# Cross-attention and FFN kernel: K and Q transformed from sums and differences of rows t and t+64, the mixing matrix filled by DMAs

## The chip, the cores and the metric

The kernel runs on one core of one Trainium2 chip. The metric is the device time of one execution in microseconds. The kernel before takes 1065.87 us (median of 3 runs, 1065.73 to 1066.18).

## The reference

x is (128, 128, 256) and the context is (128, 128, 256), both float32; 16 heads of 16 columns, `Lv` = 128.

```python
Q, K, V = (queries @ wq), (keys @ wk), (values @ wv)     # each as (B, head, Dh, L)
corr = irfft(rfft(Q) * conj(rfft(K)), n=Lv)              # along L
top_vals, top_idx = top_k(corr, 4)
w = softmax(top_vals)
out = sum_i w[i] * V rolled by top_idx[i] along Dh (mod 16)
x = x + out @ wo                  # queries = layernorm(x), keys = values = context
x = x + ffn(layernorm(x))         # 256 -> 1024 -> 256, gelu; weights rounded to 8 bits, activations to 16
```

## The kernel before

The program is written engine by engine (one block each for SyncE, TensorE, ScalarE, GpSimd, VectorE), with semaphores between them. Every engine executes its own instructions in the written order, so that order is the schedule.

The work has three stages. Stage 1 is the attention: a loop over 64 pairs of batch elements (`PAIRS`), unrolled, software-pipelined by hand: in step t each engine calls its parts for pairs t, t-1, ... t-7 (`step(t)` on each engine), and the last pairs have an order of their own, written out after the loop. Stage 2 computes the hidden layer for 32 quads, stage 3 the output layer.

In one step of stage 1 TensorE executes, for pair n: `project_k` (L455) and `project_v` (L505), `project_out` of pair n-4 (L530), `project_q` (L468), `attend` of pair n-3 (L519), `dft_k` and `dft_q` (L481, L493), `inverse` of pair n-1 (L545). Projections are exact to more than 16 bits: both operands are split into a float16 high part and a float16 rest, and three of the four products are summed (`PARTS`). ScalarE makes the high parts, GpSimd the rests (`low_ct` for the context, `low_xt` for x, `low_cs` for the spectrum, `low_ot` for the attention's output). The two transforms are float32 matmuls with a 128 x 64 part of the table, one half of the output partitions for each batch element. The product of the spectra is formed by VectorE (`products`) and GpSimd (`add_terms`), split (`high_cs`, `low_cs`) and transformed back by 24 float16 matmuls (`inverse`).

VectorE then takes the eight largest of each row and their places (`top_values`, `top_places`), makes the mixing weights (`one_hot` to `spread_weights`) and transposes them in blocks of 32 (`turn_weights`, into `blocks`). ScalarE copies the four blocks on the diagonal into the 128 x 128 matrices of `mt` (`spread_blocks`, L749), whose other blocks stay zero, and `attend` multiplies V with them. `residual` adds x; `statistics2`, `moments2` (VectorE), `scale_both` (GpSimd) and `normalize2` (ScalarE) make the second layer norm. `scale_both` makes in one go the scale of that norm for pair t-6 and the scale of the first norm for pair t-1, which `take_q_scaled` (ScalarE) applies to Q. SyncE's queue issues the loads and stores, also in order: `store_x1`, `load_x`, `load_turned`, `load_x_turned`.

Bank 1 of PSUM holds K's projection and then Q's; bank 7 holds V's projection and then the output of `attend`.

## Time and profile before

| | |
|---|---|
| median of the runs | 1065.87 us |
| span of the profiled execution (first to last instruction) | 1064.2 us |
| stage 1, loop in steady state | one step of 8.88 us for each pair |
| stage 1, order written out for the last pairs | from 554 us to 595 us |
| stage 2, stage 3 | 595 to 821 us, 821 to 1064 us |
| busy over the span: TensorE, VectorE, ScalarE, GpSimd | 1047.4, 965.1, 939.9, 505.0 us |
| granted TensorE clock | full speed throughout |

The profiled execution's own time lies within 2 us of its span; the median of the runs is 1.7 us above the span. Busy times of matmuls are those of pipelined instructions: starts of consecutive groups say more than their durations. The chain of work that ended last is 94% TensorE.

### The profile page before, as it was taken

How to read it: one execution, taken by the hardware profiler on the slowest of the kernel's cores; microseconds unless marked ns; L12 is line 12 of the kernel's file. 1: busy time of each engine (PE TensorE's matmuls, PEld its weight loads, DVE VectorE, ACT ScalarE, POOL GpSimd, SP SyncE). 2: the span in 40 equal slices, each digit the busy share in tenths (PEclk: the TensorE clock that was granted, in tenths of full speed). 3: DMA queues.
4: the chain of work that ended last, by engine and by line, in shares of the span. 5: the costliest groups of instructions: out<-in, count | busy, mean ns of one | idle time of the engine just before them, and what ended most of it. 6: DMA issues, size and time to landing. Idle time of an engine off the chain costs nothing.

```text
span 1064.2 us, 28999 instructions
## 1 busy us (share of the span) xinstructions
PE 1047.4 (98%) x9358; PEld 778.0 (73%) x9358; DVE 965.1 (91%) x2768; ACT 939.9 (88%) x1697; POOL 505.0 (47%) x674
## 2 busy tenths in 40 slices
PE   8999999999999999999998899999999999999998
PEld 6788888888888888888887444444444888888887
DVE  4789999999988888888889999999997999999998
ACT  5888888899999998888888688888888999999996
POOL 5788888888888888888887400000001000000000
PEclk9999999999999999999999999999999999999999
DMA  5454444334445443444431498999999999999995
GB/s 178 130 150 145 121 121 120 121 120 120 121 120 140 121 120 120 121 120 120 120 111 41 132 325 301 300 305 316 309 300 342 356 347 363 355 354 355 346 364 195
DMA packets 141665, 222.59 MB, mean 209 GB/s; under 512 B 72432, under 2 KB 92272, under 8 KB 137456
## 3 DMA queue, kind: packets, MB, share of 16 engines
q1 hardware_dynamic: 140464, 220.12, 62.8%
q8 instruction: 61, 1.00, 0.4%
q10 hardware_dynamic: 1088, 1.05, 0.3%
q14 instruction: 52, 0.43, 0.1%
HBM read 121.00 MB, written 83.89 MB: 193 GB/s over the span
## 4 chain that ended last, share of the span: by engine, by line
PE 94%; ACT 2%; DVE 2%; issue 1%; DMA 1%; POOL 0%; ACTq 0%; DVEq 0%; POOLq 0%
PE sums L666 21%; PE bank L635 10%; PE sums L635 10%; PE sums L464 8%; PE sums L477 8%; PE bank L515 8%; PE sums L539 7%; PE sums L489 6%; PE bank L527 5%; PE bank L501 5%; PE bank L556 5%; PE sums L672 1%; DMA store_x<-in_L_xattn_wv 1%; ACT arena L756 0%; ACT arena L686 0%
## 5 line engine op out<-in xcount | busy, mean ns | idle before, releaser
L666 PE MATMUL sums<-wout,arena 128*128 128x256 f16 x2048 | 229.8, 273 | 1.2 <-DVE arena L1521 1.2
L666 PEld LDWEIGHTS sums<-wout,arena 128*128 128x128 f16 x2048 | 196.9, 98 | 32.5 <-DVE arena L1514 7.3
L1521 DVE SCALAR_TENSOR_TENSOR arena<-arena,wout_rel 128x512 f16<-128x512 int16 x256 | 180.3, 746 | 2.0 <-ACT arena L935 0.9
L756 ACT ACTIVATE arena<-arena 32x128 f32<-32x128 f32 x256 | 78.6, 307 | 47.8 <-DVE arena L1222 45.5
L635 PE MATMUL sums<-arena,win 128*128 128x512 f16 x512 | 115.9, 379 | 1.0 <-DVE arena L1466 0.9
L635 PE MATMUL bank<-arena,win 128*128 128x512 f16 x512 | 115.7, 379 | 0.0
L686 ACT ACTIVATE arena<-arena 128x512 f16<-128x512 f32 x192 | 112.9, 617 | 1.6 <-POOL arena L998 1.1
L1485 DVE TENSOR_REDUCE hmax_all<-arena 128x1 f32<-128x1024 f32 x96 | 111.3, 1211 | 2.9 <-ACT arena L892 2.9
L935 ACT ACTIVATE arena<-arena,wout_rel 128x512 f16<-128x512 int16 x159 | 106.2, 706 | 0.0
L892 ACT ACTIVATE arena<-sums,b_in_sb,z_scale 128x512 f32<-128x512 f32 x128 | 97.4, 778 | 9.8 <-PE sums L635 4.9
L1088 POOL CAST store_x<-one 128x1 bf16<-128x1 f32 x1 | 0.2, 189 | 220.0 <-DVE one L1503 220.0
L928 ACT ACTIVATE arena<-arena,one 128x1536 int16<-128x1536 f32 x63 | 99.2, 1575 | 4.5 <-DVE arena L1521 3.0
L1010 POOL TENSOR_TENSOR arena<-arena 128x512 f16<-128x512 f32 x64 | 74.2, 1159 | 54.8 <-ACT arena L686 54.8
L1291 DVE MAX8 arena<-bank 128x8 f32<-128x128 f32 x256 | 57.1, 286 | 46.9 <-PE bank L556 46.8
L477 PE MATMUL sums<-store_x,arena 128*128 128x256 f16 x768 | 94.3, 273 | 1.0 <-ACT arena L686 0.5
L515 PE MATMUL bank<-arena,store_x 128*128 128x256 f16 x768 | 94.3, 273 | 1.0 <-ACT arena L686 0.6
L635 PEld LDWEIGHTS sums<-arena,win 128*128 128x128 f16 x512 | 50.0, 98 | 61.9 <-issue 1.4
L464 PE MATMUL sums<-store_x,arena 128*128 128x256 f16 x768 | 95.0, 273 | 0.0
L635 PEld LDWEIGHTS bank<-arena,win 128*128 128x128 f16 x512 | 50.1, 98 | 60.4
L539 PE MATMUL sums<-store_x,arena 128*128 128x256 f16 x762 | 93.7, 273 | 0.4 <-POOL arena L1006 0.4
L998 POOL TENSOR_TENSOR arena<-arena 128x512 f32<-128x512 f32 x64 | 81.4, 1272 | 3.5 <-DVE arena L1231 3.4
L477 PEld LDWEIGHTS sums<-store_x,arena 128*128 128x128 f16 x768 | 74.9, 98 | 10.4 <-issue 0.8
(141 smaller groups left out, 2303.7 us busy)
## 6 DMA issues: line engine op xcount, KB each, us to landing
hidden_scratch<-arena SPq DMA_DIRECT2D x32, 1536.0 KB, 5.5
arena<-hidden_scratch SPq DMA_DIRECT2D x64, 768.0 KB, 6.7
arena<-in_ctx_turned SPq DMA_DIRECT2D x64, 256.0 KB, 2.6
arena<-in_x_turned SPq DMA_DIRECT2D x64, 256.0 KB, 2.9
arena<-in_x SPq DMA_DIRECT2D x64, 256.0 KB, 3.7
x_scratch<-arena SPq DMA_DIRECT2D x64, 256.0 KB, 3.4
arena<-x_scratch SPq DMA_DIRECT2D x32, 512.0 KB, 6.0
out<-arena SPq DMA_DIRECT2D x31, 512.0 KB, 4.2
```

The lines of the kernel that those rows point to most:

```text
L464: last = nc.tensor.matmul(bank[1][:, b * D:(b + 1) * D], ct16[:, i, c, b * P:(b + 1) * P], w16[:, j, 3, c, :], start=c == 0 and k == 0, st ...
L477: last = nc.tensor.matmul(bank[1][:, b * D:(b + 1) * D], xt16[:, i, c, b * P:(b + 1) * P], w16[:, j, 0, c, :], start=c == 0 and k == 0, st ...
L515: last = nc.tensor.matmul(bank[7][:, e * D:(e + 1) * D], w16[:, j, 1, c, e * P:(e + 1) * P], ct16[:, i, c, :], start=c == 0 and k == 0, st ...
L539: last = nc.tensor.matmul(pair(7)[:, 1, :] if p == PAIRS - 1 and b == 1 else pair(0)[:, b, :], ot16[p % 2][:, i, c, b, :], w16[:, j, 2, c, :],
L635: last = nc.tensor.matmul(bank[f][:, :].rearrange("p (n t) -> p n t", n=4), win16[:, f, c, :], xt[q % 3][:, s, :, c, :], start=s == 0 and ...
L666: last = nc.tensor.matmul(bank[m * 2 + k // 2][:, k % 2 * D:(k % 2 + 1) * D], gbuf[:, s, f, k * P:(k + 1) * P], wout16[:, f, :], start=f = ...
L686: nc.scalar.activation(dst, src, ACT.Copy).then_inc(S[done], 1)
L892: nc.scalar.activation(dst, bank[b][:, :], ACT.Gelu, bias=b_in_sb[:, f:f + 1], scale=z_scale[:, f:f + 1]).then_inc(S[done], 1)
L928: nc.scalar.activation(hq[:, a:b, :].rearrange("p f t -> p (f t)"), src, ACT.Copy, scale=h_up).then_inc(S["c_hq"], 1)
L935: nc.scalar.activation(gbuf[:, 0, f, :], hq[:, f, :], ACT.Copy, scale=wout_rel[:, f:f + 1]).then_inc(S["c_hi_act"], 1)
L1485: V.tensor_reduce(hmax[:, bass.ds(q, 1), k], halls[m][:, 2 * k:2 * k + 2, :], AX_XY, ALU.max, apply_absolute_value=True).then_inc(S["b_max ...
L1521: V.scalar_tensor_tensor(gbuf[:, 1, f, :], hq[:, f, :], wout_rel[:, f:f + 1], gbuf[:, 0, f, :], ALU.mult, ALU.subtract).then_inc(S["c_lo"], 1)
```

## The change

1. `constants`, the layouts and the projections: the time rows of a pair's context are stored by halves (rows t and t+64). For the context, GpSimd makes sums and differences of the halves before the split (new `mix_ct`), so K's projection comes out as sums and differences already. For Q, ScalarE takes one half out of PSUM (`take_q_half`, one instruction where `take_q_scaled` had two) and VectorE makes the sum and the difference (new `mix_q`).
2. `transform` replaces `dft_k` and `dft_q`: even frequencies need only the sums, odd ones only the differences, so each matmul contracts 64 rows into 32 output partitions: 16 matmuls, in eight 64 x 32 tiles of the array, where there were 8 of 128 x 64.
3. `inverse` uses float32 operands: 8 matmuls instead of 24; `high_cs` and `low_cs` are gone.
4. `spread_blocks` is four DMAs on SyncE's queue instead of four ScalarE instructions, except for the last 5 pairs (`BY_HAND`). `mt` is laid out by groups of 32 rows; `attend` reads it in pieces.
5. Second layer norm, except for the last 5 pairs (`BY_BN`): `residual` is two instructions that also accumulate the sums, GpSimd makes the negative mean (new `minus_mean2`), ScalarE the sum of squares (new `squares`); `statistics2` and `moments2` are gone there. `scale_both` works for pair t-7, and `normalize2` and `magnitude` one step later.
6. On TensorE `project_q` stands ahead of `project_out`. `UNROLL` is 8 instead of 10.

```diff
             def load_turned(p):
-                wait(sp, S["ct_ready"], p)
+                wait(sp, S["ct_mixed"], p)
                 sp.dma_start(cturn, ctx_turned[p]).then_inc(s_t_in, 16)
+            def spread_blocks(p):
...
+                sp.wait_ge(S["bt_done"], p + 1)
+                wait(sp, S["ot_done"], p)
+                for i in range(4):
+                    part = slice(32 * i, 32 * i + 32)
+                    sp.dma_start(mt[part, i], blocks[part]).then_inc(s_mt, 16)
...
                 if active(t, 0) and t >= X_FIRST:
                     load_x(t)
+                if active(t, 5):
+                    spread_blocks(t - 5)
                 if active(t, 0) and t > 0:
                     load_turned(t)
...
-            def dft_k(p):
+            def transform(p):
...
                 pe.wait_ge(S["kf_out"], p + 1)
                 wait(pe, S["terms_done"], p)
-                for r in range(2):
-                    for b in range(2):
-                        last = nc.tensor.matmul(bank[3][b * NF:(b + 1) * NF, r * D:(r + 1) * D], dft[:, r * NF:(r + 1) * NF], kf[:, b, :],
-                                                start=True, stop=True)
-                last.then_inc(S["k_done"], 1)
...
                 pe.wait_ge(S["qf_out"], p + 1)
                 wait(pe, S["q_out"], p)
                 for r in range(2):
+                    for src, dst, turned in ((kf, 3, 1), (qf, 4, 0)):
+                        for b in range(2):
+                            rows = slice((b ^ turned) * NF, (b ^ turned) * NF + NF)
+                            for odd in range(2):
+                                strip = slice((b * 2 + odd) * 32, (b * 2 + odd) * 32 + 32)
+                                last = nc.tensor.matmul(bank[dst][strip, r * D:(r + 1) * D], dft[rows, odd * NF + r * 32:odd * NF + r * 32 + 32], src[rows, odd, :],
+                                                        start=True, stop=True)
+                last.then_inc(S["kq_done"], 1)
...
-                        for l, (i, j) in enumerate(PARTS):
-                            for b in range(2):
-                                half_of = slice(b * NF, (b + 1) * NF)
-                                last = nc.tensor.matmul(bank[5 + b][:, e * P:(e + 1) * P], cs16[half_of, i, k, e * P:(e + 1) * P],
-                                                        inv16[half_of, j, k, :], start=k == 0 and l == 0, stop=k == 1 and l == 2)
+                        for b in range(2):
+                            half_of = slice(b * NF, (b + 1) * NF)
+                            last = nc.tensor.matmul(bank[5 + b][:, e * P:(e + 1) * P], csum[half_of, k, e * P:(e + 1) * P],
+                                                    inv32[half_of, k, :], start=k == 0, stop=k == 1)
...
+            def take_q_half(p):
                 act.wait_ge(S["qp_done"], p + 1)
                 act.wait_ge(S["scales_done"], p + 1)
+                wait(act, S["qf_out"], p)
+                nc.scalar.activation(q_half, pair(1)[:, 1, :], ACT.Copy, scale=rs[(p + AHEAD) % 2][:, 1, 1, :]).then_inc(S["q_half_out"], 1)
...
+            def squares(p):
+                act.wait_ge(S["nm_done"], p + 1)
+                for b in range(2):
+                    last = nc.scalar.activation(xnt[:, p, b, :], x1[p % 2][:, b, :], ACT.Square, bias=nm[p % 2][:, b, :], scale=1.0, accum_out=mv[p % 2][:, 0, b, 1:2])
+                last.then_inc(S["ln2_stats"], 1)
...
+            def mix_ct(p):
+                pool.wait_ge(s_t_in, p * 16 + 16)
+                wait(pool, S["ct_high"], p)
+                wait(pool, S["ct_ready"], p)
+                nc.gpsimd.tensor_tensor(sd[:, :, 0:P], cturn[:, :, 0:P], cturn[:, :, P:2 * P], ALU.add)
+                nc.gpsimd.tensor_tensor(sd[:, :, P:2 * P], cturn[:, :, 0:P], cturn[:, :, P:2 * P], ALU.subtract).then_inc(S["ct_mixed"], 1)
...
+            def mix_q(p):
+                dve.wait_ge(S["q_half_out"], p + 1)
+                wait(dve, S["kq_done"], p)
+                for k, op in enumerate((ALU.add, ALU.subtract)):
+                    last = V.scalar_tensor_tensor(qf[:, k, :], pair(1)[:, 0, :], rs[(p + AHEAD) % 2][:, 1, 0, :], q_half, ALU.mult, op)
+                last.then_inc(S["qf_out"], 1)
...
-                V.scalar_tensor_tensor(x1[p % 2], pair(0), 1.0 / W_UP, xin[p % UNROLL], ALU.mult, ALU.add).then_inc(S["x1_done"], 1)
...
+                for b in range(2):
+                    last = V.scalar_tensor_tensor(x1[p % 2][:, b, :], pair(0)[:, b, :], 1.0 / W_UP, xin[p % UNROLL][:, b, :], ALU.mult, ALU.add,
+                                                  accum_out=mv[p % 2][:, 0, b, 0:1])
```

The order of instructions, at two places. On TensorE, in a step of the loop: before, from `attend` (L527) over `dft_k` (L489) and `dft_q` (L501) to `inverse` (L556). A row is a line, an operation, its tiles and the shape of its output; x3 means three more of the same.

```order
L527 MATMUL bank<-arena,store_x 128x128 [waits s_ot_out,s_vt_out,s_mt_out]
L527 MATMUL bank<-arena,store_x 128x128 x3
L489 MATMUL sums<-arena,cst 64x256 [waits s_terms_done,s_kf_out]
L489 MATMUL sums<-arena,cst 64x256 x3
L501 MATMUL bank<-arena,cst 64x256 [waits s_q_out,s_qf_out]
L501 MATMUL bank<-arena,cst 64x256 x3
L556 MATMUL bank<-inv,arena 128x128 [waits s_top_done,s_cs_ready]
L556 MATMUL bank<-inv,arena 128x128 x23
```

After, from `attend` (L544) over `transform` (L518) to `inverse` (L573):

```order
L544 MATMUL bank<-arena,store_x 128x2x64 [waits s_ot_out,s_vt_out,s_mt]
L544 MATMUL bank<-arena,store_x 128x2x64 x3
L518 MATMUL sums<-arena,cst 32x256 [waits s_qf_out,s_q_out,s_terms_done,s_kf_out]
L518 MATMUL sums<-arena,cst 32x256 x3
L518 MATMUL bank<-arena,cst 32x256 x4
L518 MATMUL sums<-arena,cst 32x256 x4
L518 MATMUL bank<-arena,cst 32x256 x4
L573 MATMUL bank<-inv,arena 128x128 [waits s_top_done,s_sums_done]
L573 MATMUL bank<-inv,arena 128x128 x7
```

The two groups of four have become four groups of four that alternate between the two banks, and they start on one set of waits: Q's operand is awaited ahead of K's transform too. `inverse` is 8 long instead of 24, and waits for `add_terms` alone.

On GpSimd, one step of the loop before: `low_ct`, `low_cs`, `low_xt`, `low_ot`, the four instructions of `scale_both` (L983 to L992), `add_terms` (L998), `take_shift`.

```order
L1010 TENSOR_TENSOR arena<-arena 128x512 [waits s_ct_high]
L1002 TENSOR_TENSOR arena<-arena 128x512 [waits s_sum_high]
L1014 TENSOR_TENSOR arena<-arena 128x512 [waits s_xt_high]
L1006 TENSOR_TENSOR arena<-arena 128x512 [waits s_ot_out]
L983 TENSOR_SCALAR arena<-arena 128x2 [waits s_ln2_stats,s_xn1_done,s_qf_out,s_ln1_stats]
L984 TENSOR_SCALAR arena<-arena 128x4
L987 TENSOR_TENSOR arena<-arena 128x4 [waits s_ln_pow]
L992 TENSOR_TENSOR arena<-arena 128x2 [waits s_ln_pow]
L998 TENSOR_TENSOR arena<-arena 128x2x256 [waits s_cs_ready,s_terms_done]
L1019 TENSOR_TENSOR arena<-arena 128x16 [waits s_exp_done,s_sc_top]
```

After: `low_ct` (L1040), `mix_ct` (L1031, L1032), `low_xt`, `low_ot`, `minus_mean2` (L991), `scale_both` (L1010 to L1018), `take_shift`, `add_terms` (L1024).

```order
L1040 TENSOR_TENSOR arena<-arena 128x512 [waits s_ct_high]
L1031 TENSOR_TENSOR arena<-arena 128x2x128 [waits s_ct_ready,s_ct_high,s_t_in]
L1032 TENSOR_TENSOR arena<-arena 128x2x128
L1044 TENSOR_TENSOR arena<-arena 128x512 [waits s_xt_high]
L1036 TENSOR_TENSOR arena<-arena 128x512 [waits s_ot_out]
L991 TENSOR_SCALAR arena<-arena 128x2 [waits s_xn1_done,s_x1_done]
L1010 TENSOR_TENSOR arena<-arena 128x4 [waits s_ln2_stats,s_xn1_done,s_qf_out,s_ln1_stats]
L1013 TENSOR_TENSOR arena<-arena 128x4 [waits s_ln_pow]
L1018 TENSOR_TENSOR arena<-arena 128x2 [waits s_ln_pow]
L1049 TENSOR_TENSOR arena<-arena 128x16 [waits s_exp_done,s_sc_top]
L1024 TENSOR_TENSOR arena<-arena 128x512 [waits s_inv_done,s_terms_done]
```

The 512-wide `low_cs` is gone and two instructions of 2 x 128 stand one place behind `low_ct`; `add_terms` and `take_shift` have changed places.

On SyncE's queue, one step after; L338 are the four DMAs of `spread_blocks`:

```order
L342 DMA x_scratch<-arena 128x512 [waits s_x1_done]
L321 DMA arena<-in_x 128x512 [waits s_x1_done]
L338 DMA arena<-arena 32x128 [waits s_ot_done,s_bt_done]
L338 DMA arena<-arena 32x128 x3
L325 DMA arena<-in_ctx_turned 128x512 [waits s_ct_mixed]
L329 DMA arena<-in_x_turned 128x512 [waits s_xt_ready]
```

They stand ahead of the load of the context (L325), which so comes behind the wait for `turn_weights` (`bt_done`).

## Rows read from the trace of the kernel before

**Rows 1.** Stretches: us; busy time (instructions) of each engine; PEclk, DMA share, GB/s
```profile
300.00:400.00 100.00, 100.00 (x1079) 82.50 (x1077) 88.85 (x368) 91.79 (x215) 85.64 (x113) 1.00 0.43 123
```

**Rows 2.** Timeline, one step, TensorE: start us, us, engine line op, shapes, xcount
```profile
305.13 1.48 PE L464 MATMUL sums<-store_x,arena 128*128 128x256 f16 x12
...
310.38 1.06 PE L527 MATMUL bank<-arena,store_x 128*128 128x128 f32 x8
...
311.37 1.08 PE L489 MATMUL sums<-arena,cst 128*64 128x256 f32 x8
...
313.25 0.84 PE L556 MATMUL bank<-inv,arena 64*128 64x128 f16 x24
...
314.02 1.49 PE L464 MATMUL sums<-store_x,arena 128*128 128x256 f16 x12
```

**Rows 3.** Timeline, TensorE, project_k of pair 3
```profile
30.04 1.48 PE L464 MATMUL sums<-store_x,arena 128*128 128x256 f16 x12
```

**Rows 4.** Timeline, TensorE, project_k of pair 62
```profile
554.14 1.48 PE L464 MATMUL sums<-store_x,arena 128*128 128x256 f16 x12
```

**Rows 5.** Timeline, the step of rows 2, VectorE
```profile
305.24 0.89 DVE L1291 MAX8 arena<-bank 128x8 f32<-128x128 f32 x4 [0.85 <-PE bank L556]
...
306.05 0.29 DVE L1222 STREAM_TRANSPOSE arena<-arena 128x128 f32<-128x128 f32 x1
...
307.44 0.08 DVE L1298 MATCH_VALUE_LOAD arena<-arena,bank 128x8 f32 x1
...
308.71 0.74 DVE L1165 BATCH_NORM_STATS2 arena<-arena 128x6 f32<-128x256 f32 x2
...
309.90 0.69 DVE L1274 TENSOR_REDUCE xmax<-store_x 128x1 f32<-128x512 f32 x1
...
310.50 0.68 DVE L1238 SCALAR_TENSOR_TENSOR arena<-sums,arena 128x512 f32<-128x512 f32 x1
...
311.22 0.75 DVE L1245 BATCH_NORM_STATS2 arena<-arena 128x6 f32<-128x256 f32 x2
...
311.89 0.42 DVE L1191 TENSOR_TENSOR sums<-sums,arena 128x256 f32<-128x256 f32 x1
...
312.21 0.24 DVE L1268 BATCH_NORM_AGGREGATE arena<-arena 128x2 f32<-128x6 f32 x2
...
314.13 0.89 DVE L1291 MAX8 arena<-bank 128x8 f32<-128x128 f32 x4 [0.85 <-PE bank L556]
```

**Rows 6.** Timeline, the same step, GpSimd
```profile
306.28 0.25 POOL L983 TENSOR_SCALAR arena<-arena 128x2 f32<-128x2 f32 x1
...
308.17 1.28 POOL L998 TENSOR_TENSOR arena<-arena 128x512 f32<-128x512 f32 x1
...
310.47 1.16 POOL L1010 TENSOR_TENSOR arena<-arena 128x512 f16<-128x512 f32 x1 [0.85 <-ACT arena L686]
```

**Rows 7.** Groups of instructions, GpSimd, one of 256 elements: busy us, mean ns
```profile
L1078 POOL TENSOR_TENSOR store_x<-b_out_sb,store_x 128x256 f32<-128x256 f32 x1 | 0.7, 671 | 0.1
```

**Rows 8.** Timeline, the same step, ScalarE
```profile
308.16 0.59 ACT L730 ACTIVATE store_x<-bank 128x512 f32<-128x512 f32 x1
...
308.78 1.09 ACT L762 ACTIVATE store_x<-arena 128x256 f32<-128x256 f32 x2
...
309.78 1.13 ACT L686 ACTIVATE arena<-arena 128x512 f16<-128x512 f32 x2
...
310.92 0.81 ACT L718 ACTIVATE arena<-sums,arena 128x256 f32<-128x256 f32 x2
```

**Rows 9.** Timeline, the same step, SyncE's queue
```profile
305.11 0.33 SPq L318 DMA_DIRECT2D arena<-in_x_turned  x1
```

**Rows 10.** DMA issues of the run: xcount, KB each, us to landing
```profile
arena<-in_ctx_turned SPq DMA_DIRECT2D x64, 256.0 KB, 2.6
...
arena<-in_x SPq DMA_DIRECT2D x64, 256.0 KB, 3.7
...
out<-arena SPq DMA_DIRECT2D x2, 256.0 KB, 2.1
```

More of the change, by code:

```diff
@@ L847, in _ @@
             take_k(PAIRS - 2)
[L848 removed]
+            normalize2(PAIRS - 8)
             exponent(PAIRS - 4)
             high_ct(PAIRS - 1)
+            take_v(PAIRS - 2)
+            take_q_half(PAIRS - 2)
+            squares(PAIRS - 7)
             high_xt(PAIRS - 1)
[L852 to L854 removed]
             take_q(PAIRS - 2)
```

298 lines of the change are left out of this document (155 added, 143 removed).

## Prediction

> **What bounds the kernel now.** I read the page first: TensorE is busy for 98% of the span and makes up 94% of the chain of waits. Then the stretches: in 100 us of stage 1 TensorE has no idle time, while VectorE is busy for 89, ScalarE for 92 and GpSimd for 86 of them, at the full clock [rows 1]. So stage 1 ends as TensorE does, and three others follow close behind. The timeline of one step shows what TensorE does in its 8.89 us: four projections from 305.13 to 310.38 (5.25), `attend` 0.99, the two forward transforms 1.88 (311.37 to 313.25), `inverse` 0.77 [rows 2]. From `project_k` of pair 3 to that of pair 62, 59 steps take 524.1 us, 8.88 each [rows 3, 4]. VectorE waits 0.85 us a step for `inverse` [rows 5], GpSimd 0.85 for ScalarE's `high_ct` [rows 6]. Stages 2 and 3 keep their instructions, so I leave their time as it is.
>
> **TensorE after the change.** `dft_k` and `dft_q` are 8 float32 matmuls of 256 columns, in pairs on two halves of the output: four rounds in 1.88 us. `attend` gives the rate: 4 float32 matmuls of 128 columns, one after another, in 0.99, so with about 0.1 for changing the array's shape 0.22 each and 0.43 for 256 columns [rows 2]. Four rounds are 1.72, and 0.16 is left for changing shape. `transform` has 16 matmuls of the same 256 columns in eight tiles: two rounds if all eight run at once, 0.86 + 0.16 = 1.02 us. Bounds: 0.9 (no cost of changing) and 1.88 (four at a time). I take 1.02, as pairs already overlap fully in the trace. `inverse`: 24 float16 matmuls in 12 rounds in 0.77; 8 float32 ones in 4 rounds of 0.22 and 0.10 make 0.99, so it gets dearer by 0.22. Sum: 5.25 + 0.99 + 1.02 + 0.99 = 8.25 us, 0.63 less than 8.88. If TensorE stayed the bound, 59 steps would give 37 us.
>
> **What each other engine gains and loses.** ScalarE loses `high_cs` (half of 1.13), one half of `take_q_scaled` (0.4 of 0.81) and the four block copies, and gets `squares`, two instructions of the size of `normalize2`'s (1.00 from start to start), with a little for the accumulators [rows 8]. It has room.
> VectorE loses `statistics2` (0.67, 311.22 to 311.89) and `moments2` (0.16, of 0.24 busy). It gets `mix_q`, two instructions of 256 columns out of PSUM; the nearest row, L1191, takes 0.42, and 0.32 to the next start: 0.70 for both, bounds 0.64 and 0.84. `residual` becomes two halves that write sums: 0.60 to 0.75 (bounds 0.65 and 1.0) [rows 5]. Its work stays at about 8.0 us a step.
> GpSimd loses `low_cs` (1.15) and gets `mix_ct`: two of 256 elements at 0.67 to 0.7 by the only row of that size, 1.38 [rows 6, 7]; bounds 1.15 (all as one of 512) and 1.6. `minus_mean2` costs little, as its multiplication stood in `scale_both`. Sum about 8.2.
> The Trainium skill (VectorE: DVE Perf Modes, Two Vector instructions with no wait between them) says that an operation that writes out its accumulator is two instructions; that speaks for the upper bounds of `residual`. No row here shows one.
>
> So with 8.25, 8.0 and 8.2 us on three engines the sums of work no longer decide. The closed loops of waits do. I look for loops that come back to the same engine one or two pairs later, and divide by the number of pairs.
>
> **Pieces of the loops**, from start to start in the trace.
> - ScalarE, from the end of `scale_both` over `normalize2` 1.00 (308.78 to 309.78), `high_ct` and `exponent` 0.62 (1.14 up to 310.92, less one copy of 0.52) and `take_q_half` 0.41, to VectorE: 2.13 with two handovers of 0.05 [rows 8].
> - `mix_q` 0.70.
> - VectorE from the end of `mix_q` to `top_values`: first norm, one-hot and magnitude 1.79 (308.71 to 310.50), of which about 0.2 is a wait (the magnitude starts at 309.90, just as `normalize2` ends at 309.87) so 1.59; `residual` and `sum_ex` 0.72 + 0.15; the rest 1.39 (311.89 to 313.28, which is 314.13 less the wait of 0.85) - 0.16 = 1.23. Together 3.70.
> - `top_values` and `turn_weights` 1.1; up to the end of `products` 2.2 (305.24 to 307.44) [rows 5].
> - GpSimd: `add_terms` 1.25, each 512-wide subtraction 1.15, `mix_ct` 1.38, `minus_mean2` 0.3, `scale_both` 1.89 (306.28 to 308.17) less the 0.3 that moved out, 1.6 [rows 6].
>
> **Loop 1**, without TensorE: `scale_both`, ScalarE 2.13, `mix_q` 0.70, VectorE 3.70 + 2.2, handovers 0.1, then on GpSimd `add_terms`, `low_ct`, `mix_ct`, `low_xt`, `low_ot`, `minus_mean2` and `scale_both` of two steps on, 1.25 + 1.15 + 1.38 + 1.15 + 1.15 + 0.3 + 1.6 = 7.98. Total 16.8 for two pairs: 8.4 us a pair.
>
> **Loop 2**, through SyncE's queue. The DMAs of `spread_blocks` wait for `turn_weights`, and `load_turned` stands behind them. One issue costs 0.33 us at its cheapest in the trace [rows 9]; I bound that of a 16 KB piece by 0 and 0.33. After four of them (1.32) the load is issued and lands after 2.6 [rows 10]. Then `mix_ct` 1.38, `low_xt`, `low_ot` 2.3, `minus_mean2` 0.3, `scale_both` 1.6, ScalarE 2.13, `mix_q` 0.70, VectorE 3.70 + 1.1, handovers 0.1. Total 17.2 for two pairs, 8.6 us; with 0.25 per issue 8.45.
>
> **Loop 3**, through the four DMAs themselves: VectorE 3.70 + 1.1, the DMAs, `attend` 0.99, `transform` 1.02, `inverse` 0.99, `project_k` and `project_v` 2.63 + 0.2, then `take_v` 0.62 (308.16 to 308.78) [rows 8], ScalarE 2.03 and 0.1, `mix_q` 0.70: 14.1 + the DMAs. The last of them is issued 1.0 after the first; the nearest landing for quick and small is 2.1 (256 KB in a quiet queue), the farthest 3.7 [rows 10]. With 3.1 it is 17.2, 8.6 us a pair; with 2.1, if the small size takes away half the landing, 8.1.
>
> The three agree on about 8.5. I take 8.55 us a pair: the DMA loops decide by a little.
>
> **The sum**, from the profiled execution's own 1065.9 us (span 1064.2 and 1.7 around it; the median of the runs is the same within 0.1):
> - 59 x (8.88 - 8.55) = -19.5.
> - Pairs 10 to 31 have an extra reduction of 256 columns on VectorE (about 0.33 each, priced like L1191). It lay under the wait of 0.85; it is now in every loop, once in two pairs: +3.
> - Start: `mix_ct` of pair 0 (1.38) comes before the first split, partly under the loads of the weights: +1 (0 to 1.5).
> - The last pairs, from 554 us on: shorter from spectrum to lags by `high_cs` and `low_cs`, longer by `mix_q` and one step more of the second norm: -0.5 (-3 to +3).
> Result 1049.9, so 1050 us.
>
> **Rivals.**
> A. TensorE stays the bound at 8.25 to 8.3 us: the loops run shorter than I sum them, as small DMAs may be issued in 0.1 and land in 1.5. For it: the three loops are over 8.3 by 0.1 to 0.3 only, 1 to 2% of their length per pair. Against it: three would have to be short at once, and jitter adds. 59 x 0.61 = -36, with +1 and -1: 1030 us.
> B. Slower: SyncE's queue becomes the bound. The load of x and the store of x1 stand just ahead of the four DMAs in the same queue, and in this traffic loads of x land after 3.7. If both the four DMAs and the load behind them land as late, loop 2 is 18.3 (9.15 a pair) and loop 3 14.1 + 1.0 + 3.7 = 18.8 (9.4). It decides against the change as soon as loop 3's DMAs take over 3.7 in all, or the load behind them over 3.1. 59 x 0.4 = +24, and 3 for the reductions: about 1090 us; half way there, 1075.
> C. The eight tiles do not run at once. Two row halves of the array write the same bank at the same time here, at different partitions, which no row shows: in `inverse` the halves write banks 5 and 6. Four at a time make `transform` 1.88 and TensorE's step 9.11: 59 x 0.23 = +14, about 1080 us. The Trainium skill (TensorEngine Tiling, Restrictions and Gotchas) says it outright: different row tiles cannot access the same PSUM bank simultaneously; by that rule this case would hold. In each half round here K's two row tiles share bank 3 and Q's bank 4, and whether the rule means banks or a bank's partitions is not shown by any row of before.
> D. The gains and the new waits cancel, within 2 us of before.
>
> **Chances.** Forecast (1036 to 1062) 0.54; A 0.17; B 0.16; C 0.06; D 0.07. A difference of 0.2%, 2 us, is about what a measurement of this kernel can tell from none. Faster by over 0.2%: forecast, A and a little of D, 0.72; within: 0.06; slower: B and C, 0.22. The range for 8 in 10 reaches from full gain at TensorE's sum to the weak half of B: 1029 to 1071 us. The forecast's own is 1036 to 1062.
>
> **What would show it.** In the profile after: `transform` about 1.0 us from start to start and `inverse` 1.0 (else C); steps of 8.5 to 8.6, TensorE idle 0.2 to 0.4 us in each, put down to `mix_q` ahead of `transform` or to the DMAs ahead of `attend`; GpSimd's `mix_ct` waiting for the load of the context, and VectorE waiting for ScalarE ahead of `mix_q` where before it waited for `inverse`. Landing of the load of the context under 3 us and of the 16 KB pieces under 2.5, else B. I am wrong in the cause, even with the right time, if TensorE shows no idle time at all in the loop, or if the four DMAs are issued and landed a microsecond before `attend`.

## The result, and the profile after

The changed kernel takes 1132.07 us (median of 4 runs, 1125.18 to 1135.8) against 1065.8 for the kernel before in the same session (1065.44 to 1066.18): a ratio of 1.0615, 95% interval 1.0579 to 1.0651. It is slower by 66 us, where I had forecast 16 us faster, and it lies outside my range. The profiled execution of after is the quickest of its four: span 1123.3 us, 59.1 more than before's 1064.2. Where these 59 us are, three starts of TensorE's rows tell (`project_k` of pairs 3 and 62 and the first matmul of stage 2, L487 and L649 in the new numbering):

```profile
33.75 1.49 PE L487 MATMUL sums<-store_x,arena 128*128 128x256 f16 x12
...
609.24 1.48 PE L487 MATMUL sums<-store_x,arena 128*128 128x256 f16 x12
...
654.36 1.89 PE L649 MATMUL sums<-arena,win 128*128 128x512 f16 x7 [0.69 <-DVE arena L1519]
```

and of before, for the third of them:

```profile
595.19 2.17 PE L635 MATMUL sums<-arena,win 128*128 128x512 f16 x8 [0.94 <-DVE arena L1466]
```

Against [rows 3, 4] pair 3 starts 3.7 us later; the 59 steps take 575.5 us instead of 524.1, 9.75 each instead of 8.88: +51.4; the last pairs take 45.1 instead of 41.05: +4.1. Stages 2 and 3 are as before.

The same stretch as [rows 1] (us, then busy time and instructions of TensorE, its weight loads, VectorE, ScalarE and GpSimd, granted clock, DMA share, GB/s), and 10 us out of it:

```profile
300.00:400.00 100.00, 87.98 (x1017) 71.00 (x1016) 78.51 (x337) 71.55 (x169) 76.89 (x109) 0.95 0.41 118
330.00:340.00 10.00, 8.25 (x88) 6.30 (x87) 6.37 (x29) 6.51 (x16) 7.83 (x12) 0.83 0.40 120
```

No engine is full any more: TensorE is busy 88 of 100 us where it was 100, and all the others have fallen too. That is how a loop of waits looks: a chain of work and waits that comes back to its own start, so that a step can't be shorter than the chain. One step of TensorE (as [rows 2]; the bracket is the idle time before the instruction and who ended it):

```profile
304.10 1.16 PE L544 MATMUL bank<-arena,store_x 128*128 128x128 f32 x8 [1.02 <-DMA arena<-arena]
305.19 0.42 PE L518 MATMUL sums<-arena,cst 64*32 64x256 f32 x4
...
306.21 1.16 PE L573 MATMUL bank<-inv,arena 64*128 64x128 f32 x16
...
307.31 1.49 PE L487 MATMUL sums<-store_x,arena 128*128 128x256 f16 x12
...
313.78 1.16 PE L544 MATMUL bank<-arena,store_x 128*128 128x128 f32 x8 [1.06 <-DMA arena<-arena]
```

`transform` (L518, eight tiles) is 305.19 to 306.21, the 1.02 us I had worked out; `inverse` is 1.10, `attend` 1.09 (0.99 before; the kernel's new reading of `mt` in pieces isn't what costs, as in e5, which has it too, an `attend` that doesn't wait takes 0.98, 423.63 to 424.61). What is new is the wait of `attend` for the DMAs that spread the weights. SyncE's queue in that step (as [rows 9]):

```profile
308.24 0.33 SPq L329 DMA_DIRECT2D arena<-in_x_turned  x1
308.62 0.91 SPq L342 DMA_DIRECT2D x_scratch<-arena  x1
309.58 0.43 SPq L321 DMA_DIRECT2D arena<-in_x  x1
310.11 2.44 SPq L338 DMA_DIRECT2D arena<-arena  x4
312.59 0.58 SPq L325 DMA_DIRECT2D arena<-in_ctx_turned  x1
```

Two results of the same trace on these DMAs: the duration of one issue (ns, least, median, most), and from issue to landing (KB each, us; as [rows 10]):

```profile
L338 SPq DMA_DIRECT2D arena<-arena x236: 507/590/720, 36.6 to 603.8; - x118
```
```profile
arena<-in_ctx_turned SPq DMA_DIRECT2D x64, 256.0 KB, 2.9
...
arena<-arena SPq DMA_DIRECT2D x236, 16.0 KB, 2.4
```

And who waits on VectorE and GpSimd, the same step (as [rows 5, 6]):

```profile
303.67 0.88 DVE L1269 SCALAR_TENSOR_TENSOR arena<-sums,arena 128x256 f32<-128x256 f32 x2 [1.30 <-ACT arena L739]
...
308.37 0.89 DVE L1345 MAX8 arena<-bank 128x8 f32<-128x128 f32 x4
309.17 0.29 DVE L1262 STREAM_TRANSPOSE arena<-arena 128x128 f32<-128x128 f32 x1
...
315.52 0.73 POOL L1031 TENSOR_TENSOR arena<-arena 128x256 f32<-128x256 f32 x1 [1.57 <-DMA arena<-in_ctx_turned]
...
316.89 1.16 POOL L1044 TENSOR_TENSOR arena<-arena 128x512 f16<-128x512 f32 x1
```

Read together, two chains stand out. The first comes back after one pair and I had not summed it: `low_xt` ends (308.22), SyncE issues the load of x turned, the store of x1, the load of x, the four DMAs (2.44) and the load of the context (312.59), which lands 2.9 later; `mix_ct` (315.52) and `low_xt` (316.89 to 318.05) follow: 9.8 us. Two of its links are tight in every one of the 59 steps with DMAs: the load of x turned is issued 0.03 us after `low_xt` ends, and `mix_ct` starts 0.07 after the load of the context lands. In 48 of them the queue's part is tight too, and the four DMAs follow the load of x; in the other 11 they follow the end of the transpose. Once around takes 9.74 us in the mean, and the mean step is 9.75. The steps themselves are 8.4 to 13.2 us long, as the landing of that load (2.5 to 3.7), the store's issue (up to 1.5) and the queue's waits for VectorE, for the transpose above all, vary.

The second is my loop 3: `turn_weights` is done at 309.46, and `attend` starts at 313.78, 4.3 us later (4.6 in the mean), where I had taken 3.1. It is long, but it isn't what holds this step: the four DMAs are issued at 310.11, 0.65 after the weights are ready, because the queue gets to them only then. It holds the steps in which the queue waits for the transpose.

### The profile page after: what moved, and what is told of

Its sections match the earlier page's. It is cut to its first block, busy times and chain, and to the rows that moved or that the text cites. A ratio compares the mean times of both kernels' runs of the same rounds, so it can differ in the third digit from the quotient of the medians.

```text
span 1123.3 us, 30275 instructions
## 1 busy us (share of the span) xinstructions
PE 1036.5 (92%) x9870; PEld 766.1 (68%) x9870; DVE 970.3 (86%) x2838; ACT 880.5 (78%) x1569; POOL 515.6 (46%) x742
## 4 chain that ended last, share of the span: by engine, by line
PE 43%; SPq 9%; DMA 7%; POOL 5%; issue 2%; DVE 1%; ACT 1%; DVEq 0%; POOLq 0%; ACTq 0%
PE sums L680 20%; PE sums L649 10%; PE bank L649 10%; DMA arena<-in_ctx_turned 7%; SPq L338 5%; POOL arena L1044 3%; POOL arena L1031 2%; SPq L342 1%; SPq L321 1%; PE sums L686 1%; SPq L329 1%; POOL arena L1032 1%; PE bank L573 0%; DMA arena<-arena 0%; PE bank L544 0%
## 5 line engine op out<-in xcount | busy, mean ns | idle before, releaser
L1269 DVE SCALAR_TENSOR_TENSOR arena<-sums,arena 128x256 f32<-128x256 f32 x128 | 56.0, 479 | 95.8 <-ACT arena L739 95.8
L544 PE MATMUL bank<-arena,store_x 128*128 128x128 f32 x512 | 73.8, 287 | 64.0 <-DMA arena<-arena 60.2
L544 PEld LDWEIGHTS bank<-arena,store_x 128*128 128x128 f32 x512 | 62.0, 191 | 80.8 <-DMA arena<-arena 76.5
L649 PE MATMUL sums<-arena,win 128*128 128x512 f16 x512 | 115.9, 379 | 0.7 <-DVE arena L1519 0.7
L649 PE MATMUL bank<-arena,win 128*128 128x512 f16 x512 | 115.7, 379 | 0.0
L700 ACT ACTIVATE arena<-sums 128x512 f32<-128x512 f32 x66 | 39.3, 598 | 85.0 <-PE sums L487 82.9
L700 ACT ACTIVATE arena<-bank 128x512 f16<-128x512 f32 (+1 forms) x130 | 77.3, 596 | 35.3 <-PE bank L544 33.0
L487 PE MATMUL sums<-store_x,arena 128*128 128x256 f16 x768 | 95.2, 274 | 0.4 <-POOL arena L1040 0.4
L649 PEld LDWEIGHTS sums<-arena,win 128*128 128x128 f16 x512 | 49.9, 98 | 61.6 <-issue 1.2
L649 PEld LDWEIGHTS bank<-arena,win 128*128 128x128 f16 x512 | 50.1, 98 | 60.4
L1031 POOL TENSOR_TENSOR arena<-arena 128x256 f32<-128x256 f32 x64 | 47.2, 737 | 91.7 <-DMA arena<-in_ctx_turned 91.7
```

The lines of the kernel that those rows point to most:

```text
L487: last = nc.tensor.matmul(bank[1][:, b * D:(b + 1) * D], ct16[:, i, c, b * P:(b + 1) * P], w16[:, j, 3, c, :], start=c == 0 and k == 0, st ...
L544: last = nc.tensor.matmul(bank[7][:, :].rearrange("p (c h b i k) -> p c h b i k", c=2, h=2, b=2, i=4)[:, c, :, b], vt[:, p, c, 1 - b, :], ...
L649: last = nc.tensor.matmul(bank[f][:, :].rearrange("p (n t) -> p n t", n=4), win16[:, f, c, :], xt[q % 3][:, s, :, c, :], start=s == 0 and ...
L700: nc.scalar.activation(dst, src, ACT.Copy).then_inc(S[done], 1)
```

## The experiments

Thirteen kernels were run. "Step" is the mean of the 59 steps from pair 3 to pair 62 of the profiled run. Each ratio is against before in the same session. e3 leaves out half of the mixing weights' blocks, and e4 and e10 put blocks at wrong places; they show time only.

| run | what differs | us | ratio (95%) | step |
|---|---|---|---|---|
| before | | 1065.8 | 1 | 8.88 |
| after | | 1132.1 | 1.0615 (1.0579 to 1.0651) | 9.75 |
| e5 | before, blocks by four DMAs | 1109.7 | 1.0422 (1.0400 to 1.0444) | 9.60 |
| e3 | after, two of the four DMAs | 1084.0 | 1.0166 (1.0149 to 1.0183) | 9.05 |
| e4 | after, one DMA, same bytes | 1075.4 | 1.0093 (1.0076 to 1.0110) | 8.86 |
| e2 | after, load of context first | 1119.7 | 1.0522 (1.0468 to 1.0575) | 9.61 |
| e12 | e2, store and load of x last | 1090.6 | 1.0221 (1.0190 to 1.0251) | 9.17 |
| e8 | x turned ahead of the spread too | 1623.9 | 1.5237 (1.5212 to 1.5263) | about 18 |
| e1 | after, copies first in ScalarE's step | 1144.6 | 1.0736 (1.0718 to 1.0754) | 10.08 |
| e6 | copies behind `take_q_half` | 1125.7 | 1.0562 (1.0544 to 1.0579) | 9.76 |
| e7 | copies for `normalize2`, that behind | 1082.9 | 1.0155 (1.0137 to 1.0172) | 9.01 |
| e13 | after, `take_q_half` early | 1125.9 | 1.0553 (1.0532 to 1.0574) | 9.78 |
| e10 | e4, `take_q_half` early | 1067.0 | 1.0009 (0.9995 to 1.0022) | 8.83 |
| e9 | copies early and `take_q_half` early | 1062.7 | 0.9968 (0.9958 to 0.9978) | 8.65 |
| e11 | e9, loads of wo a step later | 1062.3 | 0.9968 (0.9955 to 0.9981) | 8.70 |

Against what I expected of each (quoted below), e5, e10, e12 and e13 came out inside the range. The others missed: e1 by 77 us, e6 by 51, e7 by 23, e2 by 12, e4 by 10, e3 by 9, e9 by 0.7, all slower than the range; e8 by 519; and e11 gained 0.4 us where I expected 1.5 to 2.5. So the sign of each removal was mostly right, its size mostly too hopeful: behind each loop stood another.

### How many DMAs: e5, e3, e4

**e5**, this part of the change alone, in the old kernel (`mt` by groups of 32 as in after; the four ScalarE copies gone but for the last 5 pairs):

```diff
 load_x(t)
+if active(t, 5):
+    spread_blocks(t - 5)    # four sp.dma_start, as in after
 if active(t, 0) and t > 0:
     load_turned(t)
```

> The kernel before with this one part of the change: the four block copies as DMAs on SyncE's queue, at the change's place in the queue, and the mixing matrix laid out by groups of 32 rows. Theory Q: there the loop through the queue has no mix_ct (load of the context, high_ct, low_ct instead, which also wait for TensorE), so about 0.35 + 0.8 + 0.43 + 2.4 + 0.58 + 2.9 + 0.6 + 1.15 + low_cs 1.15 + low_xt 1.15 = 11.5 at most and 9 to 10 with what overlaps, and the loop over attend is 9 or more: slower than before, 1080 to 1150 us. Rival G: the DMAs alone cost nothing, 1060 to 1070 us.

It costs 44 us with nothing else changed. VectorE waits for `inverse` for 102.6 us in all (46.8 before), and `attend` for the DMAs for 26.1 (32 times). The loop through SyncE's queue that I had summed there isn't the one that the trace shows: the four DMAs are issued as soon as the weights are ready. What closes is a loop over one pair: the transpose, the four DMAs, `attend`, the two transforms and `inverse`, and then `top_values` (MAX8), which stands ahead of the next transpose on VectorE:

```profile
409.48 0.29 DVE L1240 STREAM_TRANSPOSE arena<-arena 128x128 f32<-128x128 f32 x1
409.80 2.42 SPq L337 DMA_DIRECT2D arena<-arena  x4
...
414.63 1.16 PE L549 MATMUL bank<-arena,store_x 128*128 128x128 f32 x8 [0.66 <-DMA arena<-arena]
...
418.49 0.89 DVE L1309 MAX8 arena<-bank 128x8 f32<-128x128 f32 x4 [2.01 <-PE bank L578]
...
419.30 0.29 DVE L1240 STREAM_TRANSPOSE arena<-arena 128x128 f32<-128x128 f32 x1
```

From transpose to transpose that is 9.8 us: 5.15 to `attend`, 3.86 to MAX8, 0.81 to the transpose.

**e3** leaves two of the four DMAs out, `for i in range(2)`; **e4** makes one of all the bytes:

```diff
-for i in range(4):
-    part = slice(32 * i, 32 * i + 32)
-    sp.dma_start(mt[part, i], blocks[part]).then_inc(s_mt, 16)
+sp.dma_start(mt[:, 0], blocks).then_inc(s_mt, 16)
```

> The changed kernel with two of the four small DMAs left out (the blocks of partitions 64 to 127 stay zero, so those parts of the mixing weights are missing). Theory Q, with 0.61 us of the queue for each: the loop falls by 1.2 us a pair, to 8.5, at the level of the other loops: 1045 to 1075 us. If the time of the four goes to something else in the queue than their number (waiting for the loads ahead of them to drain), two take as long as four and the time stays above 1110. Rival G: no change.

> After, with one DMA of all 64 KB of blocks into the first quarter of mt in place of four of 16 KB; the weights so stand at wrong places, and the output is not the reference's. Same bytes, same place in SyncE's queue. Theory Q2 (each DMA's issue costs 0.6 us whatever its bytes): issue 0.4 to 0.6 us in place of 2.4, step at the floor of e3, 8.5 to 8.7, time 1040 to 1065, below e3's 1084. Rival B2 (the DMAs' bytes or landing cost, not the issues): as with four, above 1100.

Two DMAs less give 48 us back, three less with all the bytes left 57. So the number of DMAs costs, not the bytes. e4's time of 1075 missed the expected 1040 to 1065: half of its steps have the 8.67 us expected, but start and end are 10 us longer than before's (pair 3 at 35.55, the last pairs 45.7 us), and many steps are longer. The issue of e4:

```profile
L336 SPq DMA_DIRECT2D arena<-arena x59: 470/471/543, 38.3 to 552.0; - x59
```

0.47 us for 64 KB, against 0.59 for one of 16 KB and 2.44 for four.

### The place in the queue: e2, e12, e8

```diff
 e2:                          e12:
-spread_blocks(t - 5)         -store_x1(t - 7)
+load_turned(t)               -load_x(t)
+spread_blocks(t - 5)         -spread_blocks(t - 5)
-load_turned(t)                load_turned(t)
                              +spread_blocks(t - 5)
                              +store_x1(t - 7)
                              +load_x(t)
                               load_x_turned(t)
```

e8 is e12 with `load_x_turned(t)` ahead of `spread_blocks(t - 5)`.

> The changed kernel with the load of the context put ahead of the four small DMAs in SyncE's queue. Theory Q: mix_ct no longer waits for its load, and what is left is the loop over attend, with the small DMAs 3.7 to 4.3 us from turn_weights to attend: (14.6 + 3.7 to 4.3) / 2 = 9.1 to 9.4 us a pair, so 1085 to 1108 us, TensorE idle ahead of attend. If the small DMAs cost only by standing ahead of the load: 8.5 a pair, 1050 us. Rival G: no change, 1125 to 1135.

> After, with SyncE's queue in another order: load of context, load of x turned, the four spreading DMAs, and behind them the store of x1 and the load of x. In e2 the spread stood behind the store and the load of x and was issued 1.05 us after the weights were ready. Theory Q2 (the two-pair loop: DMAs, attend, transform, inverse, K, ScalarE's step, mix_q, VectorE's 4.4 us): 1.0 us less a loop is 0.5 us a step, 1085 to 1105, below e2's 1120, still above before. Rival (SyncE's order does not matter any more, the four issues and the landing alone): 1112 to 1128, as e2.

> e2 with the store of x1 and the load of x behind the four spreading DMAs in SyncE's queue as well, and the load of x turned last as in after: what e8 was meant to show, without e8's mistake (there the load of x turned stood ahead of the spread, and its wait on low_xt of a later pair closed a loop of 18 us a pair). Theory: the spread is issued at once when the weights are ready, about 1 us sooner than in e2, 59 steps by 0.5 to 1.0 us, 1070 to 1095. Rival (the queue ahead of the spread costs nothing; its four issues and the landing alone do): 1112 to 1125, as e2.

e2 cuts the first loop (`mix_ct` no longer waits for a load behind the spread), but gives only 12 us: the second loop is nearly as long. Here it is closed, over two pairs as I had drawn it, with no idle time on VectorE between `mix_q` and the transpose:

```profile
400.17 1.16 PE L544 MATMUL bank<-arena,store_x 128*128 128x128 f32 x8 [1.19 <-DMA arena<-arena]
...
408.80 0.88 DVE L1269 SCALAR_TENSOR_TENSOR arena<-sums,arena 128x256 f32<-128x256 f32 x2 [1.75 <-ACT arena L739]
...
414.00 0.29 DVE L1262 STREAM_TRANSPOSE arena<-arena 128x128 f32<-128x128 f32 x1
...
418.37 1.16 PE L544 MATMUL bank<-arena,store_x 128*128 128x128 f32 x8 [0.91 <-DMA arena<-arena]
```

From `attend` over `transform`, `inverse`, the projections of K and V, ScalarE, `mix_q` and VectorE to `attend` two pairs on: 18.2 us, 9.1 a pair. In the mean of pairs 3 to 58 it is 4.6 us from the end of the transpose to `attend`, which makes (14.1 + 4.6) / 2 = 9.3 with the rest of my sum, against a mean step of 9.61.

e8 was my mistake. There each spread stands behind the load of x turned, which waits for `low_xt`; and GpSimd reaches `low_xt` only after `low_ot` of the pair spread just before, which needs that pair's `attend`. So each spread waits for the whole way round from the one before (295.73 to 313.35, 17.6 us):

```profile
303.22 1.16 POOL L1036 TENSOR_TENSOR arena<-arena 128x512 f16<-128x512 f32 x1 [7.52 <-ACT arena L700]
...
312.17 1.16 POOL L1044 TENSOR_TENSOR arena<-arena 128x512 f16<-128x512 f32 x1
...
313.35 0.33 SPq L329 DMA_DIRECT2D arena<-in_x_turned  x1
313.78 2.41 SPq L338 DMA_DIRECT2D arena<-arena  x4
...
317.43 2.08 PE L544 MATMUL bank<-arena,store_x 128*128 128x128 f32 x8 [7.54 <-DMA arena<-arena]
```

e12 takes the store and the load of x from in front of the four DMAs: 41 us less than after, 29 less than e2. Against after, the issue follows the weights sooner: 0.35 us after the transpose starts in the mean of pairs 3 to 58, where it was 0.82. Against e2 that is the smaller part. There too the median is 0.32 (in e8's expectation I had taken the 1.05 of single steps for the rule), the mean 0.52. The larger part is the landing: the median piece lands after 1.8 us where it took 2.5 in e2 and 2.4 in after, right behind two transfers of 256 KB, and from the first issue to `attend` it is 3.9 us in the mean where it was 4.35 in e2. Together 0.6 us less from weights to `attend`; over a loop of two pairs that is 0.3 a step, 18 of the 29 us. What gives the rest I can't show.

### ScalarE's order: e1, e6, e7, e13, e10, e9, e11

In e1, e6, e7, e9 and e11 `spread_blocks` is back on ScalarE for all pairs. e1 and e6 differ in its place alone; e7 and e9 also move `normalize2` behind `take_q_half`, and e9 puts `take_q_half` ahead of `exponent`. After's step is `take_k, take_v, normalize2, high_ct, exponent, take_q_half, squares, ...`:

```diff
 e1: +spread_blocks, take_k, take_v, normalize2, high_ct, exponent, take_q_half
 e6: take_k, take_v, normalize2, high_ct, exponent, take_q_half, +spread_blocks
 e7: take_k, take_v, +spread_blocks, high_ct, exponent, take_q_half, normalize2
 e9: take_k, +spread_blocks, take_v, high_ct, take_q_half, exponent, normalize2
 e10, e13 (DMAs kept): take_k, take_v, high_ct, take_q_half, normalize2, exponent
```

> The changed kernel with the four block copies on ScalarE for every pair, as before the change; no small DMAs on SyncE's queue. Theory Q (one loop a pair through SyncE's queue: low_xt, load of x turned, store of x1, load of x, the four small DMAs of 0.61 us each, the load of the context, mix_ct, low_xt): the loop falls by 2.4 us to about 7.2, other loops bound at 8.3 to 8.9 a pair, so 1030 to 1068 us, TensorE hardly idle, no drop of the clock. Rival G (GpSimd and VectorE's new work, mix_ct and mix_q, are what is too long): the step stays at 9.2 or more and the time above 1095 us.

> After, without the spreading DMAs: ScalarE copies the four 32-row blocks for every pair, but now behind take_q_half in its step, not at the step's start as in e1. Theory Q2 (one-pair loops made by the wait for the spread blocks are what costs, whoever makes the spread): with the copies behind take_q_half, mix_q no longer waits for turn_weights of the same step, so e1's loop of 10.1 us is cut into one over two pairs. ScalarE's step is then about 8.2 us of work, attend starts about 0.8 us later than the blocks of e3 allowed; step 8.4 to 8.9 us, time 1040 to 1075, over 70 us below e1. Rival G (mix_q, mix_ct and the order of VectorE and GpSimd themselves make the new kernel slow, the spread does not): stays near e1 and after, 1110 to 1145.

> After, with ScalarE's copies for every pair in the place of normalize2 (behind take_v), and normalize2 moved behind take_q_half. Theory Q2: the copies wait for turn_weights at about 0.6 us less than in e1 and stand ahead of take_q_half, so part of e1's loop (mix_q, VectorE 4.4 us, turn_weights, copies 1.3, high_ct, exponent, take_q_half) is left: 0.9 + 4.4 + 1.3 + 1.3 = about 8 us, below TensorE's own step of 8.3; the blocks are there sooner than in e6, so the step is 8.3 to 8.6 and the time 1035 to 1060, a little below e6. Rival G: 1110 to 1145.

e1 and e6 missed by 77 and 51 us, in the same way. In e1 (line numbers of that kernel) the copies wait for VectorE at the head of ScalarE's step, and `take_q_half`, for which VectorE's `mix_q` waits, is queued behind them:

```profile
311.50 1.26 ACT L769 ACTIVATE arena<-arena 32x128 f32<-32x128 f32 x4 [1.68 <-DVE arena L1264]
...
315.52 0.45 ACT L737 ACTIVATE arena<-sums,arena 128x256 f32<-128x256 f32 x1
...
316.00 0.88 DVE L1271 SCALAR_TENSOR_TENSOR arena<-sums,arena 128x256 f32<-128x256 f32 x2 [2.09 <-ACT arena L737]
...
321.53 0.29 DVE L1264 STREAM_TRANSPOSE arena<-arena 128x128 f32<-128x128 f32 x1
321.86 0.95 ACT L769 ACTIVATE arena<-arena 32x128 f32<-32x128 f32 x3 [2.02 <-DVE arena L1264]
```

That closes on itself after one pair: copies 4.0 to `take_q_half`, 0.5 to `mix_q`, 5.5 to the transpose, 0.3 back: 10.4 us in this step; the mean step is 10.08. In e6 the copies stand behind V, `take_v`, `normalize2` and `take_q_half` and `attend` waits for them (1.18 us a step): again one pair, 9.8 us. e7 is bound by a third: K starts at 405.02, V ends, `take_v`, copies, `high_ct`, `exponent`, `take_q_half`, `mix_q`, `transform`, `inverse`, and the next K 8.98 us later; 53 of its 59 steps are 8.97 or 8.98. The same chain, with `normalize2` in the place of the copies, is in after as well, below the longer loop through SyncE's queue; in e4, in steps in which nothing else binds, it is bare:

```profile
399.73 1.48 PE L485 MATMUL sums<-store_x,arena 128*128 128x256 f16 x12
...
402.56 0.60 ACT L743 ACTIVATE store_x<-bank 128x512 f32<-128x512 f32 x1 [0.71 <-PE bank L530]
...
404.67 0.46 ACT L737 ACTIVATE arena<-sums,arena 128x256 f32<-128x256 f32 x1
...
405.16 0.88 DVE L1267 SCALAR_TENSOR_TENSOR arena<-sums,arena 128x256 f32<-128x256 f32 x2 [0.73 <-ACT arena L737]
...
406.38 0.42 PE L516 MATMUL sums<-arena,cst 64*32 64x256 f32 x4 [0.23 <-issue]
```

> e4 (one DMA of all blocks, which puts the weights at wrong places), with ScalarE's step in the order take_k, take_v, high_ct, take_q_half, normalize2, exponent. Theory P: most steps of e4 are 8.67 us because take_q_half stands behind normalize2 (1.08 us) and exponent; with it ahead, the floor of the steps falls to about 8.46, and the time by 59 x 0.2 = 12 us to 1060 to 1068. Rival (the floor of 8.67 is TensorE's own work and issue gaps, or VectorE's): no change from e4, 1073 to 1078.

> After as it is, four DMAs, but ScalarE's step in the order take_k, take_v, high_ct, take_q_half, normalize2, exponent, as in e10. Theory: in after the steps of 9.75 us are set by the DMAs, and VectorE gets q_half sooner but its weights wait in SyncE's queue all the same; the loop over two pairs (spread, attend, transform, inverse, K, ScalarE to take_q_half, mix_q, VectorE) still contains the 1.3 us saved, so 0 to 0.6 us a step: 1097 to 1132. Rival (ScalarE's order is the main cause, not the DMAs): as e10 and e4, 1065 to 1080.

> After, no spreading DMAs; ScalarE copies the blocks for every pair in the idle gap between take_k and take_v, and its step goes on take_v, high_ct, take_q_half, exponent, normalize2. Theory P (the traces of e4, e6 and e7 all show a loop of one pair: projections K and V, ScalarE from take_v to take_q_half or the copies, mix_q, transform, inverse, the next K; 8.67 us in e4, 8.98 in e7, 9.80 in e6): here ScalarE needs take_v 0.6, high_ct 0.6, take_q_half 0.5 behind V, mix_q ends 5.3 us after K starts, and TensorE's four projections and attend end at 6.3, so the loop is gone and TensorE's own 5.25 + 1.09 + 1.02 + 1.10 = 8.46 is the step, 8.4 to 8.6. Against e4 (step 8.86, 1075) that is 1048 to 1062, at or below the kernel before. Rival (VectorE, 5.5 us from mix_q to turn_weights, then copies, take_v, high_ct, take_q_half: 8.4 plus hand-overs): step 8.7 to 9.0, 1065 to 1085.

> e9, with the four loads of wo on ScalarE's queue, its high half and its mixing on VectorE all one step later. In after the four issues took 2.66 us at 9.42 ahead of take_k of pair 0, and pair 3 started 3.7 us later than before. Theory: 1.5 to 2.5 us less than e9. Rival (the start is set by the short pipeline, take_q_half, mix_q and transform one behind the other): same as e9 within 0.5 us.

e10 shows the floor: with `take_q_half` ahead of `normalize2` its shortest and commonest step is 8.35 to 8.36 (29 of 59) where e4's commonest is 8.67 to 8.68 (also 29); the 8 us less are about 59 x 0.31 = 18 less what longer steps take back (those in which `attend` waits for the DMA, up to 2.8 us). e13 makes the same edit with four DMAs: 6 us, so in after ScalarE's order is a small part, and in these runs a barely measured one (after's own spread over 10 us). e9 removes both causes and beats the kernel before by 3.2 us, 0.3%, with a mean step of 8.65. The range that I gave it, 1048 to 1062, it just missed. Most steps of its last 30 are 8.46 or 8.47, and in one of them one sees VectorE's loop that I had given as the rival (copies wait for the transpose by 0.16), with TensorE idle for hardly 0.1 between `attend` and `transform`:

```profile
523.07 0.29 DVE L1265 STREAM_TRANSPOSE arena<-arena 128x128 f32<-128x128 f32 x1
523.39 1.26 ACT L769 ACTIVATE arena<-arena 32x128 f32<-32x128 f32 x4 [0.16 <-DVE arena L1265]
...
526.36 1.06 PE L542 MATMUL bank<-arena,store_x 128*128 128x128 f32 x8
...
527.46 0.42 PE L516 MATMUL sums<-arena,cst 64*32 64x256 f32 x4
```

Pairs 10 to 31, in which VectorE and ScalarE also prepare the weights of stages 2 and 3, mostly take 8.8 (the prediction had counted 3 us for them); there the extra work is no longer hidden. And pair 3 starts 6.1 us later than before, the end takes 3.1 us longer. e11 brings pair 3 forward by 2.7 us (33.48), but pair 62 starts at the same time as in e9 (546.64 and 546.52), and the times are the same, where I had expected 1.5 to 2.5 us: what a start gains is lost again later in stage 1.

## Why the prediction was wrong, by its own steps

**TensorE after the change** was nearly right: `transform` 1.02 as worked out, `inverse` 1.10 for 0.99, `attend` 1.09 for 0.99. Its step is then 5.25 + 1.09 + 1.02 + 1.10 = 8.46 by the starts in after, and 8.35 to 8.36 in the commonest steps of e10, against 8.25. So 0.4 to 0.5 us a step were to be had, not 0.63. Rival C is refuted: K's row tiles share a bank, and all eight ran at once: four at a time would have taken 1.88. The Trainium skill's rule (TensorEngine Tiling (Array Packing), Restrictions and Gotchas) that different row tiles cannot use one PSUM bank at a time does not hold here for tiles that write different partitions of it: 16 matmuls of 256 columns took 1.02 us.

**The pieces of the loops** were right: ScalarE from `normalize2` to `mix_q` 2.11 (311.10 to 313.21) for 2.13; VectorE from the end of `mix_q` to `top_values` 3.9, with 0.3 of weight preparation in it, for 3.70; `mix_ct` 1.38 for 1.38; `mix_q` 0.79 from start to start for 0.70.

**The step that failed is loop 2's and loop 3's price of the DMAs**: "I bound that of a 16 KB piece by 0 and 0.33". The median issue is 0.59, and four take 2.44 us of SyncE's queue, where loop 2 had 1.32; the last is issued 1.8 us after the first, where loop 3 had 1.0. The row I took (0.33) was the cheapest issue in the queue; the sum needed a bound above it, as the loads of x in the same trace show 0.43. The landing, on the other hand, was close: 2.4 us in the median where loop 3 had 2.1. With the queue's delay ahead of them, from the ready weights to `attend` it is 4.3 us, not 3.1: loop 3 becomes (14.1 + 4.3) / 2 = 9.2 us.

Rival B, which had 0.16, named the right place, SyncE's queue, but another cause: that the pieces and the load behind them land late, at 3.7. They landed after 2.4 and 2.9, so by my own sign ("landing of the load of the context under 3 us and of the 16 KB pieces under 2.5, else B") the trace would have spoken against B, while the time was beyond it. That sign was a bad one: it looked at the landing and not at the issue. Of the other signs, `transform`, `mix_ct`'s wait for the load and VectorE's wait for ScalarE came as written, but TensorE's idle time ahead of `attend` is 1.0 us a step in the mean, where I had 0.2 to 0.4. B's price was also too low by its own numbers: its longer loop of 9.4 gives 59 x 0.52 = 31 and a time of about 1100, not 1090.

The Trainium skill (DMA: Bandwidth & Descriptors, Rules for kernel authors) advises one 128-partition transfer in place of two on disjoint halves of the partitions; the measured 0.47 for one against 2.44 for four agrees in direction, though that advice speaks of the DMA engines that both halves share and not of the time of an issue.

**The second error was the kind of loop I looked for.** All three of my loops ran over two pairs. In e2 it was indeed my loop 3, in the stretch shown. But those that set the pace of most runs ran over one: through SyncE's queue in after (9.75), from transpose to transpose in e5 (9.8 in the step shown), through ScalarE's queue in e1 (10.1) and e6 (9.8), through ScalarE, `mix_q` and `transform` in e7 (8.98) and e4 (8.67). `mix_q` stands on a new path from ScalarE over VectorE back to TensorE; before, ScalarE fed the transform directly. Each of these loops joins two instructions of the same pass through the loop by the order of a queue, not by data, which is why adding up data dependences did not find them. The two errors worked together: with my price of 1.32 for the four issues the loop through SyncE's queue, 9.8 us in the step shown, would be about 8.7, close to what I had forecast; with the true price and my loops alone the forecast would have been 9.2.

**Start and end**: +3.7 and +4.1 for my +1 and -0.5. At the start `take_k` of pair 0 stands behind four DMA issues of wo on ScalarE's queue (before, wo came by one of 0.37 us; the change splits it by halves of the rows), and with few pairs under way `take_q_half`, `mix_q` and `transform` run one behind the other:

```profile
9.42 2.66 ACTq L713 DMA_DIRECT2D store_x<-in_L_xattn_wo  x4
...
12.87 1.47 PE L500 MATMUL sums<-store_x,arena 128*128 128x256 f16 x12 [2.55 <-ACT arena L700]
```

I had counted `mix_ct` there and put the issues at nothing; with them a step later pair 3 starts 2.7 us sooner (e11 against e9). Why the end is longer I did not take apart; it is longer by 2 to 5 us in every variant of the changed kernel that I looked at, with DMAs or without (e4 45.7, e9 44.1), but not in e5, the old kernel (40.8), so it comes with the other parts of the change.

**How the 66 us divide.** With one DMA in place of four 57 are gone (e4); with `take_q_half` early 8 more (e10); copies on ScalarE in the right gap give 4 more (e9), and that is 3 us below the kernel before. The order of removal matters: ScalarE's order alone is worth 6 (e13), and queue order alone 41 (e12), because each loop hides the others. The medians differ by 66 us and the profiled runs by 59; after's own runs spread over 10 us where before's lie within 0.8. Only the quickest of them has a trace, so which steps grow in the others isn't known.

## What to carry to other kernels

Price a DMA issue as an instruction of the engine that issues it, with a row of the same shape or a bound above the nearest one, and count everything that is queued behind it: here four cheap-looking issues took 2.44 us of an idle-looking queue and cost 44 us by themselves (e5). When an edit lets an engine sit between two others, walk each in-order queue once around: a wait that stands ahead of what its own releaser needs next closes a loop over one pair, and each pair then takes the whole length of that loop, where one over two pairs costs half of its length. Before judging the idea, try the order: the same arithmetic, with the same four copies on ScalarE, gave 1145, 1126, 1083 and 1063 us in four orders of that engine's step.
